# A two-layer decoder on one core: scores that wait for two maxima instead of four, weights opened by the sync engine, two moves in the experts' stages, and zeros between the cosine stage's products

## The reference

```
x = x + self_attention(layernorm(x))            # 16 heads of 8, causal
x = x + cross_attention(layernorm(x), context)  # 16 heads of 8, logits clipped
x = x + experts(layernorm(x))                   # 8 experts, the best 2 of each row, hidden 512, gelu
x = x + attention_over_batch(layernorm(x))      # 16 heads of 64, softmax over the 16 sequences
x = x + cosine(layernorm(x), context)           # see below
x = x + quantised_mlp(layernorm(x))             # blocks of 16 rounded to an FP4 grid, 352 hidden

def cosine(v_in, t_in):
    v = v_in @ Wv.T + bv                        # 16 x 128 x 64
    t = t_in @ Wt.T + bt
    dots = einsum('bih,bjh->bij', v, t)
    return dots / maximum(norm(v)[:, :, None] * norm(t)[:, None, :], 1e-8)
```

## Time and profile before

| what | value |
|---|---|
| median of 3 runs | 781.2 us (780.96 to 782.8) |
| the profiled execution | 781.81 us, span 779.9 us, mean clock 0.893 |
| PE busy / weight loads | 634.5 us (81%) / 460.4 us (59%) |
| DVE, ACT, POOL busy | 460.8, 377.6, 266.1 us |
| self tiles 24 to 158 us: PE, DVE, ACT, POOL busy | 121.61, 74.49, 83.38, 39.29 us of 134.00 |
| cross tiles 158 to 294 us: the same | 120.53, 103.84, 86.08, 48.73 us of 136.00 |
| cosine stage 667 to 703 us: the same | 29.10, 18.68, 11.85, 12.34 us of 36.00, clock 0.50 |

### The profile page before, as it was taken

How to read it: one execution, slowest core, us unless ns; L and a number is a source line. 1 busy time by engine, 2 the same in 40 slices (tenths; PEclk the granted TensorE clock), 3 DMA queues, 4 the chain that set the end, 5 groups by cost and what they waited for, 6 DMA issues and landing times. The chain is left out here.

```text
span 779.9 us, 17100 instructions
## 1 busy us (share of the span) xinstructions
PE 634.5 (81%) x6403; PEld 460.4 (59%) x6435; DVE 460.8 (59%) x1247; ACT 377.6 (48%) x817; POOL 266.1 (34%) x369
## 2 busy tenths in 40 slices
PE   3799998988999974348999985989999997685776
PEld 2455555555666553325999952667878685363555
DVE  3466655478788865752444325475757573555994
ACT  5566674868676722125444465635353523323342
POOL 3133223344344210752455562041313131143641
PEclk9799999999999995555999997999999999556898
DMA  3022344333112111116466622300000000000000
GB/s 101 2 60 67 85 103 128 90 95 78 52 40 83 62 41 46 49 42 198 169 215 216 221 54 56 86 1 2 2 2 3 1 3 2 0 1 0 8 20 27
DMA packets 53023, 48.95 MB, mean 63 GB/s; under 512 B 10219, under 2 KB 45533, under 8 KB 52685
## 3 DMA queue, kind: packets, MB, share of 16 engines
q1 hardware_dynamic: 46925, 41.09, 17.7%
q0 software_dynamic: 2496, 4.27, 1.7%
q10 hardware_dynamic: 3520, 2.50, 1.2%
HBM read 18.68 MB, written 15.54 MB: 44 GB/s over the span
## 5 line engine op out<-in xcount | busy, mean ns | idle before, releaser
L573 ACT ACTIVATE ptx<-bank 128x512 f32<-128x512 f32 x128 | 66.1, 602 | 90.7 <-PE bank L486 90.6
L1576 POOL COPY ptx<-over_pt 32x512 f32<-32x512 f32 x64 | 39.0, 610 | 132.9 <-DVE over_pt L1546 130.1
L1141 POOL DMA_INDIRECT results<-moe_y,moe_dest x46 | 45.3, 984 | 59.1 <-DVE moe_y L1279 51.1
L386 POOL TENSOR_TENSOR x<-x,l_back 128x128 f32<-128x128 f32 x32 | 14.6, 456 | 125.0 <-ACT l_back L586 113.9
L727 DVE SCALAR_TENSOR_TENSOR ptx<-ptx,bank 128x512 f32<-128x512 f32 x64 | 41.1, 684 | 25.5 <-PE bank L495 23.7
L482 PE MATMUL bank<-ke 32*128 32x512 f32 x256 | 37.4, 652 | 18.6 <-issue 14.9
L712 DVE TENSOR_REDUCE l_m<-bank 128x4 f32<-128x512 f32 x64 | 40.9, 679 | 19.4 <-PE bank L470 19.4
L1476 ACT ACTIVATE ke<-bank 64x512 f32<-64x512 f32 x64 | 38.0, 593 | 15.1 <-PE bank L1407 14.2
L1136 POOL DMA_INDIRECT slots<-xs,moe_pos x32 | 32.3, 1010 | 28.7 <-DVE moe_pos L1222 18.6
L712 DVE TENSOR_REDUCE l_m_raw<-bank 128x4 f32<-128x512 f32 x64 | 40.7, 674 | 0.1
L1450 PE MATMUL bank<-over_ot,over_wo 128*128 128x128 f32 x256 | 34.4, 290 | 6.0 <-DVE over_ot L1552 6.0
(11 more groups left out here) (347 smaller groups left out, 1662.4 us busy)
## 6 DMA issues: line engine op xcount, KB each, us to landing
slots<-blank SPq DMA_DIRECT2D x16, 528.0 KB, 4.7
ptx<-w SPq DMA_DIRECT2D x12, 578.0 KB
ke<-w SPq DMA_DIRECT2D x11, 578.0 KB, 3.3
w<-in_w SPq DMA_DIRECT2D x16, 256.0 KB
moe_xb<-slots SPq DMA_DIRECT2D x23, 132.0 KB
x<-in_x SPq DMA_DIRECT2D x4, 256.0 KB, 5.3
w<-results SPq DMA_DIRECT2D x4, 256.0 KB, 6.0
w<-results ACTq DMA_DIRECT2D x4, 256.0 KB, 5.8
```

The source lines that it names most:

```text
L573: nc.scalar.activation(probs[t % 2][:, g, :], score_bank[g][:, :], ACT.Exp, scale=SCALE0).then_inc(s["probs"], 1)
L1141: nc.gpsimd.indirect_dma_start(M.results, bass.IndirectOffsetOnAxis(dest[j % 4][:, n:n + 1], 0), y[j % 4][:, n, :], None, bounds_check=2 * ...
L1576: nc.gpsimd.tensor_copy(ptx[t % 2][r, :, r], pt[t % 2][r, :, :]).then_inc(s["spread"], 1)
```

## The change

The line numbers of the changed kernel are 7 to 28 higher. In the first attentions `scores(t)` waits for two of the four maxima of tile t+1, and the first floor of a cross tile, which writes bank 0, waits for all four:

```diff
@@ scores(t)
-                    wait(pe, s["maxed"], min(t + 1, N - 1), per=NG, plus=NG)
+                    wait(pe, s["maxed"], min(t + 1, N - 1), per=NG, plus=2)
@@ floors(t, groups)
                         if g == 0:
                             wait(pe, s["lrow"], t - B, per=16, plus=16)
+                            wait(pe, s["maxed"], min(t + 1, N - 1), per=NG, plus=NG)
```

In the opening SP issues the weights between the first and the second quarter of x, ACT takes the first scales by one square root, and DVE by one reciprocal; `prepare_row` moves:

```diff
@@ sync engine
+                load_input(0)
+                M.self_weights.load(sp, d, s["weights"])
+                for q in range(1, 4):
+                    load_input(q)
+                sp.wait_ge(s["prepared"], 4)
@@ scalar engine
-                M.self_weights.load(act, d, s["weights"])
                 act.wait_ge(s["consts"], 32)
                 W = M.self_weights
+                prepare_row(0)
+                act.wait_ge(s["var0"], 1)
+                nc.scalar.activation(root[:, 0:4], var[:, 0:4], ACT.Sqrt).then_inc(s["root0"], 1)
                 nc.scalar.activation(W.identb[:, :], ident[:, :], ACT.Copy).then_inc(s["prepared"], 1)
-                roots(0, 0)
@@
-                    if t in (-3, -2):
-                        prepare_row(t + 3)
+                    if t == -1:
+                        prepare_row(1)
@@ vector engine
-                scales(0, 0)
+                dve.wait_ge(s["root0"], 1)
+                nc.vector.reciprocal(rstd[:, 0:4], root[:, 0:4]).then_inc(s["ready0"], 1)
```

Some waits between operations of one engine on the first scales go too (plus=k in place of plus=1). In routing the high parts go into ACT's loop over q, the low parts ahead of DVE's wait for `cnorm`; in the sums `over(q)` goes ahead of `low(q-1)`:

```diff
@@ scalar engine, loop over q
+                    if q > 0:
+                        nc.scalar.activation(M.over_hi[:, q - 1, :], M.over_w[:, q - 1, :], ACT.Copy).then_inc(s["high"], 1)
@@ scalar engine, behind cnorm
-                for n in range(3):
-                    nc.scalar.activation(M.over_hi[:, n, :], M.over_w[:, n, :], ACT.Copy).then_inc(s["high"], 1)
@@ vector engine
+                for n in range(3):
+                    dve.wait_ge(s["high"], n + 1)
+                    V.tensor_tensor(M.over_lo[:, n, :], ...).then_inc(s["low"], 1)
                 dve.wait_ge(s["cnorm"], 1)
@@ vector engine, experts' sums
                     add(q)
+                    over(q)
                     if q > 0:
                         low(q - 1)
-                    over(q)
```

In the cosine stage PE multiplies zeros (a tile of 128x512 in bfloat16 that DVE clears at the stage's start) into bank 5, two products at two places of each of the ten turns of its loop; the sums of both parities now share bank 4, so `sums(u)` waits for the root of u-1 where it waited for that of u-2:

```diff
+                def keep_busy(n):
+                    pe.wait_ge(s["filler"], 1)
+                    for _ in range(n):
+                        nc.tensor.matmul(filler_bank[:, :], filler[:, 0:128], filler[:, :], start=True, stop=True)
@@ sums(u, p)
-                    wait(pe, s["norm"], u, plus=-1)
+                    wait(pe, s["norm"], u)
@@ loop over u
                         turn(u + 2, u % 2)
+                    keep_busy(2)
                     if valid(u + 1, N):
                         project(u + 1, (u + 1) % 2)
+                    keep_busy(2)
```

More of the change, by code:

```diff
@@ L607, in roots @@
                     nc.scalar.activation(log[:, r], var[:, r], ACT.Ln).then_inc(s[f"ln{k}"], 1)
-                    wait(act, s[f"ln{k}"], g, plus=1)
+                    wait(act, s[f"ln{k}"], g, plus=k)
                     nc.scalar.activation(root[:, r], log[:, r], ACT.Exp, scale=-0.5).then_inc(s[f"root{k}"], 1)
@@ L677, in scales @@
                     nc.vector.scalar_tensor_tensor(square[k][:, :], root[:, r], -0.5, root[:, r], ALU.mult, ALU.mult).then_inc(s[f"square{k}"], 1)
-                    wait(dve, s[f"square{k}"], g, plus=1)
+                    wait(dve, s[f"square{k}"], g, plus=k)
                     nc.vector.tensor_tensor(slope[k][:, :], square[k][:, :], var[:, r], ALU.mult).then_inc(s[f"slope{k}"], 1)
-                    wait(dve, s[f"slope{k}"], g, plus=1)
+                    wait(dve, s[f"slope{k}"], g, plus=k)
                     nc.vector.scalar_tensor_tensor(rstd[:, r], slope[k][:, :], 1.5, root[:, r], ALU.add, ALU.mult).then_inc(s[f"ready{k}"], 1)
@@ L1325, in _ @@
                 V.reciprocal(cinv[:, :], cfloor[:, :]).then_inc(s["cinv"], 1)
-                for n in range(3):
-                    dve.wait_ge(s["high"], n + 1)
-                    then(V.tensor_tensor(M.over_lo[:, n, :], M.over_w[:, n, :], M.over_hi[:, n, :].bitcast(F32), ALU.subtract))
                 turned(0)
@@ L1643, in cosine_block @@
         s = semaphores(nc, "cos", """variance root rstd xn xt_ps xt vt_ps vt sq sum_ps norm floored inverse
-            limited dot_ps cosine x_done stats aggr""")
+            limited dot_ps cosine x_done stats aggr filler""")
         N = B // 2
@@ L1708, in roots @@
                     wait(act, s["floored"], u, plus=-1)
[L1709 removed]
+                    nc.scalar.activation(norm[p][:, :], sum_bank[p], ACT.Sqrt).then_inc(s["norm"], 1)
                 def turned(u, p):
```

16 lines of the change are left out of this document (10 added, 6 removed).

## The result

The changed kernel takes 754.3 us (752.53 to 755.35, four runs) against 781.24 us (780.96 to 782.8). The ratio is 0.9649, 95% interval 0.9624 to 0.9674: 27 us faster. The forecast was 757.8 in 750 to 771. The profiled execution has a span of 751.7 us at a mean clock of 0.914, 28.2 us less than before.

What follows compares the result with a forecast made beforehand. PE was taken as the bound, its holes as path, and the cosine stage as PE at half clock. Gains 15 + 1.4 + 2 + 1.5 + 3.5 = 23.4 off the profiled 781.8 gave 758.4, 757.8 as median; range 750 to 771.

Steps and rivals of the forecast that it cites:

- the cases counted as faster: Whole kernel: the forecast, chance 0.78; another wait replacing the fourth maximum, 0.12; zeros not lifting the clock, 0.08.
- Scores: 15 forecast: Attention tiles: PE's 18.6 us idle before the scores closes when two maxima are awaited; 15 us gained, ends 10 and 18.
- The deduction behind it, 3.6 us: Attentions: taken off the 18.6 us, 2.1 for waits on `l_cb` and 1.5 for small waits appearing elsewhere.
- The 1.5 for new small waits: Attentions: 1.5 us taken off for waits on DVE's output part and the rows' DMAs, asked for sooner.
- The rival of another wait: Attentions: queries, exponentials or DVE's output part nearly as late; a third of the 15 comes, 767.8 us; chance 0.12.
- Opening: 1.4 forecast: Start of kernel: PE's first instruction moves from 11.16 to 9.75; 1.4 us gained, ends 0 and 2.
- the landing of the weights: Opening: last weights issued eighth on SP at about 4.5, landing 5.2 us later at 9.7, which PE awaits.
- Routing: 2 forecast: End of routing: DVE's copy starts 2.4 us earlier, no longer behind three subtractions; 2 us gained, ends 0 and 2.5.
- Sums: 1.5 forecast: Experts' sums: shift before subtraction starts ACT's normalisation about 1.0 earlier every round; 1.5 us gained, ends 0.7 and 1.8.
- Cosine: 3.5 forecast: Cosine stage: zeros raise PE's clock within one round; 6.6 gained less 2.6 and 0.5, so 3.5 us; ends 0 and 6.
- the first rival: Cosine stage: the zeros don't lift the clock; 14.5 us lost in place of 3.5 gained, 775.8 us; chance 0.08.
- the round: Cosine stage: a round costs 3.66 / 2 + 4 x 0.22 = 2.71 us at full clock, in place of 3.66.

Runs made afterwards that it cites:

- the pair on one chip: The changed kernel and the kernel before, both as they are, run again on another chip: 758.26 against 783.93 us, ratio 0.9671.
- the kernel whose zeros had ended at 643.2: Changed kernel with low-part subtractions in the loop over blocks, cosine zeros two at each place in the first three turns, none later: 745.09 us, ratio 0.9613.

## Why the prediction was right, and where it was not

The direction and the range were right and the mechanism of each of the five parts held, and the scores are the largest part by far, as forecast. Among the small ones the order was wrong: the cosine stage was to bring most and the opening least, and the opening brought most. The forecast lay 3.5 us above the measured time; the terms were off by more than that, in both directions, and partly cancelled. (One slip in the working: the chances of the cases counted as faster add up to 0.98, not 0.96.)

**Scores: 15 forecast, 20.6 measured.** The step from the row's 18.6 us of idle to the whole hole being closed held (17.5 us of it went), and so did the reading that the fourth maximum lets PE go, though the profile booked it under "issue": with three maxima awaited, steady tiles are as short as with two. The deduction behind it, 3.6 us, was mis-sized and wrongly reasoned. I took 2.1 us off for the waits on `l_cb`, because that transfer would not come earlier. It did come earlier, about as much as PE: the product that waited for it until 163.77 starts 16 us sooner (timeline of PE, changed kernel):

```profile
147.61 0.33 PE L442 MATMUL bank<-ident,l_cb 128*128 128x128 f32 x1 [1.26 <-DMA l_cb<-in_ctx]
```

I had argued from what stands ahead of it on SP's queue, and not that the queue itself advances by what PE has done. The sum of these waits grew by 0.2 us in the first pair of traces (2.1 to 2.3) but by 2.0 in the pair on one chip (2.7 to 4.7), so the size set for it was wrong in one pair and right in the other. The 1.5 for new small waits did not appear: PE's other waits between the first and the last scores sum to 2.7 us before and 2.6 after. What was missing altogether is the clock. In the kernel before, the hole of 2.31 us ahead of the first scores was followed by products at 0.50; with the hole at 1.10 that tile took 7.22 us in place of 10.61, of which only 0.37 was idle time ahead of the next scores: 3.0 us from the clock. In tile 16 PE worked at 0.56 after its wait for `l_cb`, and at 1.00 in the changed kernel (windows, before and after):

```profile
166.00:169.00 3.00, 3.00 (x54) 2.64 (x58) 2.80 (x7) 0.71 (x2) 1.15 (x2) 0.56 0.95 253
```

```profile
149.00:152.00 3.00, 3.00 (x78) 2.28 (x74) 3.00 (x8) 1.54 (x5) 1.97 (x3) 1.00 0.48 124
```

Tile 16 took 11.02 us before and 8.99 after: 1.6 us by the clock, the rest is the shorter first wait. In the other direction the last tile's values ran at 0.50, 1.4 us lost. The two traces agree with this count: between the first and the last scores PE's busy time fell from 233.2 to 228.8 us, 4.4, with no work taken away, and its idle time by 16.0. The first tile's part comes in every kernel with the hole of 1.10 (7.22 or 7.23 us in nine of them, 10.61 and 10.58 in the two traces of the kernel before). The other two are not the edit's for certain: with the short tiles tile 16 took 8.89 to 9.48 us in eight traces but 11.12 and 11.35 in two, and the last tile lost its 1.4 us in four and not in the other six. So part of the 20.6 is luck of this execution; in the pair of traces on another chip the same stage gained 19.9. The rival of another wait did not come: the queries and exponentials were in time.

**Opening: 1.4 forecast, 2.1 measured.** ACT's chain was timed well (root at 8.15 where I had 8.7 for its end), and the mechanism held. The term that failed is the landing of the weights, set at 9.7: PE started at 9.10 directly behind the first normalised tile, so the weights had landed by then. The page has the last of them (changed kernel):

```profile
self_bo<-in_self_bo SPq DMA_DIRECT2D x1, 64.0 KB, 4.0
```

It was issued at 4.14, where I had 4.5, and took 4.0 us in place of 5.2, so it landed at about 8.1. I had used the landing time of a transfer that had all four quarters of x issued ahead of it; now three of them stand behind it. That this order made it shorter is likely, not tested.

**Routing: 2 forecast, 1.7 measured**, but of two terms: the copy now comes 0.73 us behind PE's first transpose where it came 3.23 behind it (2.5 gained, 2.4 forecast), and the transposes themselves come 0.8 us later, counted from routing's start, because the scatter is held up by 1.6, about half of which the fetch had as slack. I had the second as an end of the range and not in the sum. In the pair of traces on another chip it was 0.9 instead of 1.7, and on a chip without the stalls the balance is zero.

**Sums: 1.5 forecast, 1.8 measured.** Rounds of DVE shrank from 3.71 to between 3.4 and 3.6 us and the last low part ends 1.8 us sooner: 1.1 in the last step from one subtraction to the next and 0.7 in the two before it, as worked out (1.04 and two or three times 0.25). DVE's wait for the high part, 0.94 and 1.09 us before, is 0.20 at most in the first three rounds.

**Cosine: 3.5 forecast, 1.9 measured.** The clock rose 3.8 us after PE's first transposes (643.42 to about 647.2), so the first rival falls. The term that failed is the round: 3.00 us, not 2.71. Half of 3.66 for the stage's own work was nearly right: the rounds without zeros take 2.03 us, and so the own work does not quite halve (1.83 was assumed). Start to start at full and at the lower clock: the transposes 0.37 and 0.62 us, the projection 0.57 and 1.05, the sums 0.47 and 0.87, the products 0.61 and 1.13. The zeros take about 0.24 each in this mix ((3.00 - 2.03) / 4), 0.31 with one at each place, not 0.22, which I had halved from the lower clock. Both together make the 0.29 us a round, 2.0 in seven rounds; the start cost 0.4 less than was set for it.

The sum, 23.4 against 28.1, thus hides +5.6, +0.7, -0.3, +0.3 and -1.6. Of the largest, 3.2 is the clock in the attentions (3.0 + 1.6 - 1.4), for which the sum had no term, and the rest the deductions that did not come.

## What to carry to other kernels

When an engine's idle time has no named releaser, compare the distance from candidates' ends in two kinds of tiles: the same 0.1 us in both named the maximum here, and waiting for two of the four maxima in place of all freed nearly the whole hole. Count with a hole what the clock does behind it, and prefer the earlier of two possible waits when tiles are uneven. When products are added to hold the clock, try how few still hold it, keep them to the end of the stage, and put the first into a wait that exists anyway; here half of them, and four ahead, took the stage from 30.4 to 26.0 us. A long operation moved into an idle stretch of one engine can still slow a neighbour that runs beside it; and a gain read in one trace of one chip, as in routing here, can be gone on the next.

## What the runs showed of the hardware

- PE may be busy without a gap and still not raise its clock: 10.00 us of 10.00 at 0.50 in the kernel before, 18.00 of 18.00 in the kernel without zeros. In the kernel whose zeros had ended at 643.2 the clock fell from 1.00 to 0.50 at about 650.5, with PE busy up to a gap of 0.42 us at 650.4; the gap and the missing zeros are not separated. The stage's own products have one column, use half of the rows or columns, or are transposes. The Trainium skill (TensorE: Matmul & The Clock Gate, Part 4: PE-mode transpose) says that transposes do not count as busy in the same way; no run here separates transposes from the other narrow products.
- A hole of 1.10 us before the first scores left the clock at 1.00; one of 1.71 us and one of 2.31 us were followed by 0.50. All three were in the same place; 1.10 and 2.31 were each seen with the old opening and with the new one.
- DVE subtractions of 128x1024 took POOL's scatter instructions beside them from 0.96 to 1.57, 1.81 and 1.97 us, though not every one: in the kernel with the scores' edit alone one took 1.41 and the next, beside the third subtraction, 0.96. In all kernels three earlier scatter instructions take 1.22, 1.55 to 1.56 and 1.56 to 1.73 us, beside DVE operations on 128x768 in the traces read. What they share the runs do not show.
- DVE stalled 9.0, 6.4 or 0 us in routing, by chip, with a releaser that the profile calls remote. That is not explained.
